# Two macaron layers on eight cores: the last head pair by query quarters, its output product begun early, layer 1's first weights loaded early

## The reference

```python
x = x + 0.5 * L0_ffn(layernorm(x))    # fake-quantised FFN: w1, depthwise conv, silu, w2
x = x + L0_attn(layernorm(x))         # 16 heads of 64, softmax, output product + b_o
x = x + 0.5 * L0_ffn(layernorm(x))
x = x + 0.5 * L1_ffn(layernorm(x))    # gate softmax over 8 experts, p > 0.3, experts, out_W
x = x + L1_attn(layernorm(x))         # causal linear attention: M += v k^T, y = M q, then Wo
x = x + 0.5 * L1_ffn(layernorm(x))
```

```python
q, k, v = split(x @ W_qkv.T)
weights = softmax(q @ k.T / 8)        # per head, 2048 x 2048
out = (weights @ v) @ W_o.T + b_o
```

## Time and profile before

| | us |
|---|---|
| median of 3 runs | 3297.43 (3294.39 to 3298.57) |
| the profiled execution | 3289.77 |
| its slowest core, 2 (span) | 3288.2 |
| its fastest core, 4 | 3220.6 |
| core 2: TensorE matmul busy | 2702.8 |
| core 2: VectorE busy | 2002.8 |
| core 2: ScalarE busy | 1683.9 |

### The profile page before, as it was taken

One profiled execution on the slowest core, in us unless ns is written; L12 is line 12 of the kernel. 1 busy time (PEld: TensorE's weight loads), 2 busy tenths in 40 slices (PEclk: granted clock), 3 DMA queues, 4 the chain that ended last, 5 costly groups with the idle time before them and its releaser, 6 DMA issues.

```text
span 3288.2 us, 38755 instructions; the slowest of 8 cores (3220.6 to 3288.2 us)
## 1 busy us (share of the span) xinstructions
PE 2702.8 (82%) x11557; PEld 1162.6 (35%) x11770; DVE 2002.8 (61%) x2866; ACT 1683.9 (51%) x1983; POOL 376.5 (11%) x437
## 2 busy tenths in 40 slices
PE   2557788994799999999999865597979769798789
PEld 1223333441334444444433222243434334344334
DVE  5777777754677777777754036777777324434433
ACT  5868665643226666666644715575755223414430
POOL 0000011123100011000000000011111302312210
PEclk9779998997889999998955987698989879999999
DMA  8546432326120332021100271132322360010001
GB/s 257 164 145 217 125 123 81 101 93 171 20 45 7 56 55 43 11 43 36 36 7 14 49 242 52 39 118 69 125 69 91 106 208 1 1 40 12 0 10 68
DMA packets 152760, 259.10 MB, mean 79 GB/s; under 512 B 36928, under 2 KB 72784, under 8 KB 152240
## 3 DMA queue, kind: packets, MB, share of 16 engines
q1 hardware_dynamic: 119872, 199.47, 19.7%
q0 software_dynamic: 32688, 57.13, 7.8%
HBM read 220.70 MB, written 52.56 MB: 83 GB/s over the span
## 4 chain that ended last, share of the span: by engine, by line
PE 62%; DVE 14%; ACT 8%; issue 8%; DMA 6%; POOL 1%; SPq 1%; DVEq 0%; ACTq 0%; POOLq 0%
PE fb L1140 11%; PE fb L910 8%; PE aups L1614 8%; PE apps L1728 7%; PE asps L1709 7%; PE mb L2227 6%; PE ajps L1578 3%; DVE fbig L951 2%; PE rs L2118 2%; ACT fbig L946 2%; PE mb L2282 2%; PE mb L2026 2%; DVE fbig L955 1%; DMA fbig<-w1h 1%; DVE amx L1625 1%
## 5 line engine op out<-in xcount | busy, mean ns | idle before, releaser
L1625 DVE TENSOR_REDUCE amx<-aups 128x1 f32<-128x512 f32 x1024 | 662.9, 687 | 267.5 <-PE aups L1614 265.6
L1718 ACT ACTIVATE aet<-asps 128x1024 bf16<-128x1024 f32 x512 | 521.2, 1024 | 309.0 <-PE asps L1709 306.7
L910 PE MATMUL fb<-fxsc,fw1r 128*128 128x512 bf16 x1995 | 547.1, 412 | 104.4 <-DVE fbig L955 76.5
L1140 PE MATMUL fb<-fbig 128*128 128x512 bf16 x2003 | 488.8, 390 | 56.2 <-ACT fbig L1101 29.0
L1614 PE MATMUL aups<-ahd 65*128 65x512 bf16 x1024 | 384.7, 420 | 22.7 <-DVE amx L1625 9.1
L1728 PE MATMUL apps<-aet,avt 128*65 128x512 bf16 x1024 | 344.3, 420 | 15.6 <-ACT aet L1718 10.1
L910 PEld LDWEIGHTS fb<-fxsc,fw1r 128*128 128x128 fp8e4 x2048 | 211.3, 105 | 408.3 <-issue 214.8
L1709 PE MATMUL asps<-ahd 65*128 65x512 bf16 x1024 | 344.2, 422 | 2.2
L951 DVE SCALAR_TENSOR_TENSOR fbig<-fb,cw2sb,fbig 128x511 f32<-128x511 f32 x256 | 191.4, 748 | 217.4 <-ACT fbig L946 215.2
L1140 PEld LDWEIGHTS fb<-fbig 128*128 128x128 fp8e4 x2048 | 203.4, 100 | 312.9 <-issue 87.6
L946 ACT ACTIVATE fbig<-fb,cbsb,cw2sb 128x512 f32<-128x512 f32 x256 | 195.9, 769 | 198.9 <-PE fb L910 187.5
(11 more groups left out here) (262 smaller groups left out, 2965.4 us busy)
## 6 DMA issues: line engine op xcount, KB each, us to landing
fw1r<-wq SPq DMA_DIRECT2D x224, 128.0 KB, 2.2
fbig<-wq SPq DMA_DIRECT2D x112, 256.0 KB, 2.7
fbig<-w1h SPq DMA_DIRECT2D x32, 512.0 KB, 12.7
fbig<-w2h SPq DMA_DIRECT2D x28, 512.0 KB, 3.9
fxq<-x SPq DMA_DIRECT2D x8, 1024.0 KB, 8.9
fw2f<-w2h SPq DMA_DIRECT2D x32, 256.0 KB, 4.3
fbig<-w2h SPq DMA_DIRECT2D x32, 256.0 KB, 4.1
fbig<-x POOLq DMA_DIRECT2D x32, 256.0 KB, 5.1
```

The lines of the kernel that those rows point to most:

```text
L910: tp = T(lambda e, dc=dc: e.matmul(bank[b][:, :], sl[:, o + dc * 128:o + (dc + 1) * 128], xr[:, dc * 512:(dc + 1) * 512], start=(dc == 0), ...
L1140: tp = T(lambda e, j=j: e.matmul(bank[2 + j][:, :], w2r[s][:, o + j * 128:o + (j + 1) * 128], xi2[:, hc * 512:(hc + 1) * 512], start=(hc = ...
L1625: lambda e, hh=hh, c=c: e.tensor_reduce(m[:, c:c + 1], ups[hh][:, :], axis=AX.X, op=ALU.max),
L1718: ta = A(lambda e: e.activation(et[g % 3][:, :], sps[s][:, :], AF.Exp, scale=0.125), wait=[tp, tk.get(("ef", g % 3))])
```

## The change

1. **Last pair by quarters.** In pass 7 the groups go quarter by quarter, both heads of a quarter in turn. After each quarter `last_pair` sends its channels to `ao`, two matmuls with a 65 x 128 selector spread the two heads' denominators over 128 partitions of `ups[0]`, and VectorE takes a reciprocal of 128 x 512 and multiplies 128 x 512 of `ao`.
2. **Early output product.** `wo` and all 32 residual tiles (into buffers that are free by then) are loaded at the end of pass 5. `g_wo` issues `ec` 0 to 4 of all 32 tiles in passes 6 and 7 through bank `jps`, and VectorE adds bias and residual. `g_rest` issues `ec` 5 to 7 from group 40 of pass 7 on, through banks `ups[1]` and `jps`; VectorE adds, and stores go out on GpSimd's queue.
3. **Early layer 1 weights.** Two buffers are shared between the stages; `owb` and `e0b` are loaded into them on SP's queue at the start of step q == 4 of the second FFN. The gate weights are loaded with the constants at program start.
4. **`center`** issues GpSimd's subtractions two tiles ahead, and `g_prep_m` and `g_prep_a` yield after every second tile.

`ffn` and `attn_l0` change places in the file. `keep` and `stored` only collect tokens that nothing uses.

```diff
@@ build_program
+        gw_sb = sb("lgw", [128, DC * NE], F32)
+        sh_a = sb("sha", [128, DC * QT], F32)
+        sh_b = sb("shb", [128, 2 * DC * QT], BF16)
...
+        const_tag = em.go("gpsimd", lambda e: e.dma_start(
+            gw_sb[:, :].rearrange("p (a m) -> p a m", a=DC),
+            gwT.ap().rearrange("(a p) m -> p a m", p=128)), dma=s_const)
...
+        def early_l1(w_a, w_b):
+            for key, dst, src, w in (("ow", sh_a[:, :].bitcast(BF16), owb,
+                                      w_a),
+                                     ("e0", sh_b[:, :], e0b, w_b)):
+                early[key] = em.go(
+                    "sync", lambda e, dst=dst, src=src: e.dma_start(
+                        dst.rearrange("p (a b) -> p a b", a=DC),
+                        src.ap().rearrange("(a p) m -> p a m", p=128)),
+                    wait=[pre[src.name]] + list(w), dma=s_early[key])
@@ attn_l0
-                def seq(g):
+                def seq(t, g):
+                    if t == 7:
+                        return (g // 8) % 2, g // 16, g % 8
                     return g // 32, (g // 8) % 4, g % 8
...
+                V(lambda e: e.memset(sel[:, :], 0.0))
+                V(lambda e: e.memset(sel[64:65, 0:64], 1.0),
+                  wait=[(Sdv, Sdv.c)])
+                tk["sel"] = V(lambda e: e.memset(sel[64:65, 192:256], 1.0))
...
+                def last_pair(hh, qb, ta):
+                    base = hh * 64
+                    c = slice(qb * 512, (qb + 1) * 512)
+                    o = ao[:, 7 * T + qb * 512:7 * T + (qb + 1) * 512]
+                    r = rbc[1][:, c]
+                    tk["ao7", qb, hh] = dget(
+                        s_a7[qb % 2][hh],
+                        ao[base:base + 64, 7 * T + qb * 512:7 * T + (qb + 1) * 512],
+                        stg[hh][0:64, c],
+                        wait=[ta, tk["xln", 3], tk.get(("n7", qb - 2))])
+                    tk["st7", qb, hh] = ta
+                    if hh == 0:
+                        return
+
+                    def inv():
+                        for h in range(2):
+                            tp = P(lambda e, h=h: e.matmul(
+                                ups[0][:, :], sel[:, h * 128:(h + 1) * 128],
+                                stg[h][0:65, c], start=(h == 0),
+                                stop=(h == 1)),
+                                wait=[tk["st7", qb, h], tk["u0f"],
+                                      tk["sel"]], mark=(h == 1))
+                        tk["u0f"] = tk["r7"] = V(
+                            lambda e: e.reciprocal(r, ups[0][:, :]),
+                            wait=[tp, tk["norm", 5]])
+
+                    def norm():
+                        tk["n7", qb] = V(lambda e: e.tensor_tensor(
+                            o, o, r, ALU.mult),
+                            wait=[tk["r7"], tk["ao7", qb, 0],
+                                  tk["ao7", qb, 1]])
+                    after(1, inv)
+                    after(3, norm)
...
+                EA = 5
+                def g_wo():
+                    for n, (qb, dc) in enumerate(idx):
+                        for ec in range(EA):
+                            tp = wo_mm(jps[:, :], n, ec, 0, EA - 1,
+                                       [tk["wo"], tk["norm", ec]] +
+                                       ([tk["jf"]] if ec == 0 else []))
+                            if ec < EA - 1:
+                                yield
+                        t = V(lambda e, n=n, dc=dc: e.scalar_tensor_tensor(
+                            res[n], jps[:, :], bo_sb[:, dc:dc + 1], res[n],
+                            ALU.add, ALU.add), wait=[tp, rl[n]])
+                        tk["jf"] = tk["res", n] = t
+                        yield
+
+                def g_rest():
+                    n = 0
+                    for qb in range(4):
+                        while (("n7", qb) not in tk or
+                               ("norm", 6) not in tk or
+                               ("res", 31) not in tk):
+                            yield
+                        for dc in range(DC):
+                            i = n % len(rings)
+                            for ec in range(EA, DC):
+                                tp = wo_mm(rings[i], n, ec, EA, DC - 1,
+                                           [tk["n7", qb] if ec == 7
+                                            else tk["norm", ec]] +
+                                           ([rt.get(i)] if ec == EA
+                                            else []))
+                                if ec < DC - 1:
+                                    yield
+                            t = V(lambda e, i=i, n=n: e.tensor_tensor(
+                                res[n], rings[i], res[n], ALU.add),
+                                wait=[tp, tk["res", n]])
+                            rt[i] = t
+                            dget(s_so, x_dst[dc * 128:(dc + 1) * 128,
+                                                 qb * QT:(qb + 1) * QT],
+                                 res[n], wait=[t], eng="gpsimd")
+                            n += 1
+                            yield
...
-                        pull(p, 2 if g % 8 == 0 else 1)
+                        if t < 6:
+                            pull(p, 2 if g % 8 == 0 else 1)
+                        elif t == 6:
+                            pull(p, 2 if g >= 12 else 0)
+                        elif g < 40:
+                            pull(p, 2 if g % 5 < 2 else 1)
+                        else:
+                            if g == 40:
+                                for _ in p:
+                                    pass
+                                rings = [ups[1][:, :], jps[:, :]]
+                                rt[0], rt[1] = tk["u1f"], tk["jf"]
+                                rest = g_rest()
+                            pull(rest, 2)
                         tick()
...
-                    if t == 6:
+                    if t == 5:
                         for ec in range(DC):
                             tk["wo"] = dget(
...
+                        for n in range(32):
+                            res_load(n)
                 while later:
+                    pull(rest, 3)
                     tick()
+                for _ in rest:
+                    pass
@@ ffn
+                    if q == NQ and not first:
+                        early_l1([ln["xqfree"]], ln["xscfree"])
@@ layer1
-                tk["gw"] = dget(s_g, v3(gw[:, :], DC), gwT.ap().rearrange(
-                    "(a p) m -> p a m", p=128))
+                tk["ow"], tk["e0"] = early["ow"], early["e0"]
                 x_load(0)
-                w_load("ow", s_w[0], ow[:, :], owb, DC)
-                w_load("e0", s_w[1], xs[0][:, :], e0b, DC)
                 w_load("e1", s_w[2], xs[1][:, :], e1b, DC)
...
+                    for k in range(2):
+                        sub(k)
+                    for k in range(DC):
+                        yield k, out[k]
+                        if k + 2 < DC:
+                            sub(k + 2)
...
                         tk["cf", k % 3] = t
+                        if k % 2 == 1 and k < 7:
+                            yield
```

974 lines of the change are left out of this document (486 added, 488 removed).

## The result

The changed kernel is faster: the ratio of its time to the time before is 0.9736, with a 95% interval from 0.9714 to 0.9758. Its profiled execution took 3207.2 us and two others 3208.9 and 3213.1, against 3294.4 to 3298.6 before.

A forecast was written before the change was run, and what follows sets the result against it. The bound was taken as the slow cores' low TensorE clock in pass 6. For core 2, -21 + 18.5 - 50 - 21 - 18 + 0.5 = -91 us, from 3297.4 to 3206; 8-in-10 range 3168 to 3262.

The forecast's parts named there:

- The bound and its cause: In pass 6 the slow cores are bound by TensorE's low clock; too few matmuls over 128 rows bring it back.
- Pass 6: Head pair 6 of attention, with the early output product: 144 us against 165 on core 2, so -21.
- Pass 7: Last head pair: extra matmuls, a 5 us TensorE stall at group 32, and bank waits; 77.5 to 96 us, +18.5.
- two ring estimates: Pass 7's loop between exponential and scores, with extra matmuls: 84.4 us (+11, taken) or 95.6 (another +11, the bound), against 73.3.
- Tail: From pass 7's last exponential to the second FFN's first load: 76.8 us becomes 27, -50.
- Layer 1's start: With both weights loaded early, gate matmuls start at 2634.6 and fusion at 2638.2 instead of 2659.1: -21 us.
- The early loads' cover: Second FFN: 4 MB of early loads could delay the w2 loads; four loaded slots cover 14 us, nothing charged.
- Centring: Centring products, two per yield: two thirds of 27.6 us of waits go, -18 (bounds -5, -28); waits for L2330, L2411 halve.
- A: Low clock stays in pass 6: that pass takes 211 us, +67 on the sum, total 3273 us; chance 0.12.
- B: Slower than before: low clock holds through pass 7 too, 153 us instead of 96, total 3336; chance 0.03.
- C: No slow core: all cores enter pass 6 at full clock, total 3189 us, at bounds 3179 or 3168; chance 0.15.
- D: Passes 6 and 7 cost more, by 11 (ring) and 15 (one bank, late `wo`): total 3232 us; chance 0.2.

## Why the prediction was right, step by step

**The bound and its cause: right, and now shown.** The low clock of pass 6 was what made the slow cores slow, and my reading, that matmuls over 128 rows bring it back, has held for the return: two 128-row fillers, one, one in two groups, a 128 x 65 filler and the early output product brought every low core back, the 65-row filler and the bare pass none of the five and four that were low at group 12. Not everything fits the plain form of it. Cores 5 and 6 of the 65-row kernel, and cores 5 and 6 of the changed one, fell at pass 6's start and came back after 10.2 us on the pass's own mix, before group 12; core 4 of before did so in the middle, after 6.8 us. And the return came anywhere from 0.2 us ahead of the recorded start of the first one added at group 12 (0.07 to 0.15 us on one core in each of four kernels) to 3.5 behind it, so the trace doesn't tell how many of them it takes. What is shown is what the engine did before the clock rose, not how the chip decides it. The prediction had also only one kind of slow core. Cores don't enter the pass low but fall some 1.8 us into it (core 3 of the changed kernel at 1633.1, the pass starting at 1631.3), and the three cores of before with passes of 130 to 131 us fell in the middle. Why a core falls at one of these places, and another beside it doesn't, stays open.

The Trainium skill ("TensorE: Matmul & The Clock Gate", Part 1) ties the clock to how busy the array has been. With "busy" read as the busy share of a profile the traces disagree: 40 of 40 us at 0.50 and 40 of 40 us at 1.00 in one run of the 65-row filler kernel.

**Pass 6: right.** 144 us for a core that enters low, measured 140.2 to 141.9 (34.1 or 30.7 us at half clock, where 31 and a return of 7 were summed); 129 for one that enters at full clock, measured 127.9 on the one core of the changed kernel's order without any half clock, in the run with the loads in four pieces. The clock is back sooner than the 7 us taken. Costed at nothing and not quite so: on three of the four cores that are at full clock at group 12 the first loads come late (core 2 of the changed kernel waits 2.54 us for the first of `wo` and 4.22 for the first eviction, which waits for its residual), and the clock falls for 3.4 to 10.2 us in all. So the two that had not fallen at the pass's start, cores 0 and 2, took 133.4 and 136.8 us instead of 129.

**Pass 7: mechanism right, +22 instead of +18.5.** The hole stood at group 32 as drawn. What the sum lacked was the clock: the engine fell to half clock in the hole, and paid again. Without the hole the pass takes 94 to 97; the early and the last products cost 17 to 18 there instead of 14, nearer the lower of the two ring estimates than the bound.

**Tail: right.** 27.0 and 27.3 us for 27 summed; 0.91 us a product for 0.9.

**Layer 1's start: mechanism right, -15 instead of -21.** The term set the gate matmuls at the time of the first load. They begin 6.2 us after it, although nothing they read is late; with the loads put back it is 6.1, and before it was 5.1. That lag stood in the rows, and my sign that fusion would start within 5 us of the first load failed with it: it is 9.6. The trace gives no releaser for it ("issue"), so what TensorE does there stays open.

**The early loads' cover: the step that was wrong.** "Four slots already loaded, of 16 matmuls (3.5 us) each, cover 14 us" counted the time that a slot lasts, not how long the load behind two of 2 MB takes. It came too late by 6.7 us on core 3 (and the 64 matmuls behind it took 16.8 us for core 4's 14.0, at a clock fallen in the wait), by 0.4 on core 4: up to +9.4 us on the slowest core, costed at nothing.

**Centring: mechanism right, -22.0 on core 2 instead of -18,** inside the bounds. Of the 27.6 us counted not two thirds went but half, 14.3, as the sign said. The rest came from waits that the term left out: from the fused weights to the end TensorE of core 2 wasn't busy for 65.8 us before and 42.7 after, and one of the waits that went was 7.7 us more for L2330, by the matmuls of L2363.

**The sum.** For core 2 I had -91 and it is -86: pass 6 was 7.3 us better than its term, which was that of a core that enters low (it didn't fall at the start and lost only 10.2 us at half clock), centring 4, an earlier start of the pass 2; the FFN was 8.8 worse, layer 1's start 6.1, pass 7 3.2. For core 3 I had -72.5 and it is -48: pass 6 10.8 worse, as it fell at the pass's start this time, the FFN 9.4, layer 1's start 7.9, tail 3.6, pass 7 3.3; its earlier start gave 8.0 and centring 2.4. So the near hit of the total rests in part on misses that cancel, and those 7.3 us are luck: which cores fall at the pass's start is not the same from one execution to another. In before they were 0, 2, 6 and 7, in the kernel with 128-row fillers, which is the same up to group 12, all eight. Luck aside, "core 2's kind stays the slowest" was wrong in name: all cores now pass through pass 6 within 10 us of each other, and the wait in the FFN decides which is last. Rivals A and B did not occur. C did not, as every core had some half clock in pass 6. Of D's 26 us, the ring took 3 to 4 instead of 11, and the late `wo` and residuals were waits of 2.5 and 4.2 us on core 2; the rest was not there.

## What to carry to other kernels

Compare a stage's mix of matmul shapes, not only its busy share, when the granted clock stays low: here unread matmuls over 128 rows, which compute nothing, gave back 1.2% of the whole kernel, and matmuls that had to be done anyway, moved there, brought the clock back too. Look where a stream of full-height matmuls runs out before its stage does, as the projections did seven groups before the end of each pass. A load hoisted into a busy stage needs cover for the loads queued behind it, so split it and put the pieces where their buffers come free; and price a stall of a few us with the clock that falls behind it.

## What the runs showed of the hardware

- With 65-row matmuls added TensorE stayed at a granted clock of 0.5 for 206 us on five cores, at a busy share of 100%; with the same number over 128 rows, also with only 65 columns of weights, it was back at 1 within 0.2 to 3.5 us of the first of them (first filler on core 3 at 1669.2, half clock until 1672.6). Three cores went through the 65-row pass at full clock but for 0 to 10.2 us at its start: the same work can run at either level.
- Without fillers all four cores that were at full clock at group 12 fell in the middle of the pass, three for 77 to 79 us of it and one for 6.8; with 65-row fillers none of three did.
- The fall itself costs little where it is short: 13.7 and 17.1 us at half clock at a pass's edges make passes of 113 and 115 us out of 107.
- Two loads of 2 MB issued together landed after 17.9 and 30.1 us in the FFN, beside its own loads; the two pieces of 1 MB of the second weight, one in each of two passes, in 7.4 us (median) without holding anything up.
